# Which heads' row maxima are computed a stage ahead in a four-batch decoder layer

## The reference

```python
Q = (decoder_input @ W_q).reshape(B, Sd, HEADS, HEAD_DIM)      # 16 heads of 16
K = (encoder_output @ W_k).reshape(B, Se, HEADS, HEAD_DIM)
V = (encoder_output @ W_v).reshape(B, Se, HEADS, HEAD_DIM)
scores = jnp.einsum('bqhd,bkhd->bhqk', Q, K) / jnp.sqrt(jnp.float32(HEAD_DIM))
attn = jax.nn.softmax(scores, axis=-1)                         # maximum over 512 keys, per query
out = jnp.einsum('bhqk,bkhd->bqhd', attn, V).reshape(B, Sd, E)
return out @ W_o + b_o
```

## Time and profile before

| | |
|---|---|
| median of 3 runs | 544.41 us (543.29 to 546.53) |
| the profiled execution | 544.57 us |
| its span | 542.8 us |
| VectorE, ACT, POOL busy | 71%, 54%, 40% |
| stage 0 (first exponential to that of the next) | 98.5 to 209.0 us |
| stage 1 | 209.0 to 324.1 us |
| stage 2 | 324.1 to 424.3 us |
| stage 3 | 424.3 to the end of its slots near 512 us, then the tail |

### The profile page before, as it was taken

One profiled execution on the slowest core, in us unless ns is written; L12 is line 12 of the kernel. 1 busy time (PEld: TensorE's weight loads), 2 busy tenths in 40 slices (PEclk: granted clock), 3 DMA queues, 4 the chain that ended last, 5 costly groups with the idle time before them and its releaser, 6 DMA issues. The chain is left out here.

```text
span 542.8 us, 6272 instructions
## 1 busy us (share of the span) xinstructions
PE 458.3 (84%) x1931; PEld 188.2 (35%) x1931; DVE 384.6 (71%) x640; ACT 292.3 (54%) x516; POOL 215.4 (40%) x213
## 2 busy tenths in 40 slices
PE   8997889889795978899878889888988878787984
PEld 3432523324231213353332323443422332233453
DVE  4888878673777696577997896798557668732385
ACT  4145440552754563845757656546866434687434
POOL 5559793720358575321678772422000011000000
PEclk9999989988989889999999989998989978999998
DMA  7566460621758206034755032220501410000011
GB/s 219 212 178 168 141 174 4 154 56 33 189 135 209 62 17 150 19 79 120 174 139 123 0 95 73 80 58 3 147 19 37 90 50 2 2 0 2 1 39 40
DMA packets 26512, 47.33 MB, mean 87 GB/s; under 512 B 5456, under 2 KB 16368, under 8 KB 26480
## 3 DMA queue, kind: packets, MB, share of 16 engines
q1 hardware_dynamic: 23360, 39.86, 27.6%
q10 hardware_dynamic: 3120, 7.08, 5.3%
HBM read 35.19 MB, written 9.96 MB: 83 GB/s over the span
## 5 line engine op out<-in xcount | busy, mean ns | idle before, releaser
L1529 DVE TENSOR_REDUCE MX<-bank 128x1 f32<-128x512 f32 x256 | 166.5, 681 | 108.1 <-PE bank L637 103.3
L1138 ACT ACTIVATE PT<-bank 128x512 f32<-128x512 f32 x256 | 147.0, 597 | 121.7 <-PE bank L646 111.2
L637 PE MATMUL bank<-KS,QS 96*128 96x512 bf16 x240 | 93.6, 397 | 38.0 <-DVE MX L1529 28.3
L646 PE MATMUL bank<-QS,KS 99*128 99x512 bf16 x256 | 97.9, 393 | 19.6 <-ACT PT L1138 17.9
L1830 POOL TENSOR_TENSOR W<-qT,W 128x512 f32<-128x512 f32 x48 | 61.6, 1287 | 37.6 <-DVE W L1446 26.0
L660 PE MATMUL bank<-PT,Vs 128*32 128x512 f32 x512 | 73.5, 648 | 1.5 <-ACT PT L1138 0.8
L646 PEld LDWEIGHTS bank<-QS,KS 99*128 99x128 bf16 x256 | 24.2, 98 | 106.1 <-issue 53.3
L637 PEld LDWEIGHTS bank<-KS,QS 96*128 96x128 bf16 x240 | 23.6, 98 | 98.9 <-DVE MX L1529 62.0
L1861 POOL TENSOR_TENSOR MP<-MX,zero 128x16 bf16<-128x16 f32 x15 | 4.4, 292 | 115.7 <-DVE MX L1529 76.0
L1816 POOL TENSOR_TENSOR W<-kT,W 128x512 f32<-128x512 f32 x32 | 45.3, 1419 | 6.7 <-ACT kT L993 6.7
L1446 DVE TENSOR_TENSOR_SCAN W<-bank,W 128x512 f32<-128x512 f32 x32 | 38.7, 1210 | 0.0
(11 more groups left out here) (216 smaller groups left out, 707.2 us busy)
## 6 DMA issues: line engine op xcount, KB each, us to landing
W<-v_rows SPq DMA_DIRECT2D x12, 512.0 KB, 6.3
W<-v_rows ACTq DMA_DIRECT2D x12, 512.0 KB, 6.4
k_parts<-parts SPq DMA_DIRECT2D x24, 128.0 KB, 2.4
KS<-k_parts SPq DMA_DIRECT2D x16, 192.0 KB, 3.6
q_parts<-parts SPq DMA_DIRECT2D x24, 128.0 KB, 2.6
QS<-q_parts SPq DMA_DIRECT2D x16, 192.0 KB, 3.6
cT<-in_cT SPq DMA_DIRECT2D x4, 512.0 KB, 3.9
xtok<-in_x SPq DMA_DIRECT2D x4, 512.0 KB, 5.5
```

The source lines that it names most:

```text
L637: pe.matmul(bank(n)[:, :], QS[0:NS, h, i * P:(i + 1) * P], KS[0:NS, h, :], start=True, stop=True).then_inc(filled(n), 1)
L646: pe.matmul(bank(name)[:, :], KS[0:NR, h, kt * P:(kt + 1) * P], QS[0:NR, h, :], start=True, stop=True).then_inc(filled(name), 1)
L1138: act.activation(PT[:, n % 2, j, :], bank(name)[:, :], ACT.Exp).then_inc(emptied(name), 1)
L1529: dve.tensor_reduce(MX[:, NT * h + i:NT * h + i + 1], bank(n)[:, :], AX.X, ALU.max).then_inc(emptied(n), 1)
```

## The change

Before, LAG = 6 heads of the next batch had their maximum tiles in slots 10 to 15 of the stage ahead; the other ten had them in slots 0 to 9 of their own. In stage 0 the heads 4 to 15 had them there, since the prologue makes those of heads 0 to 3 only. After, LAG = 4: heads 0 to 3 in slots 10 to 14 of the stage ahead, and heads 4 to 15 in slots 0 to 9 of every stage, dealt as in stage 0 before.

```diff
-LAG = 6
+LAG = 4
...
-NEXT_MAXIMA = dealt("o", 10, (2, 4, 4, 4, 5, 5), range(LAG))
-MAXIMA = {s: {**dealt("b", 0, (4, 5, 6, 5, 6, 2, 5, 2, 3, 2), range(LAG, H)), **NEXT_MAXIMA} for s in STEPS}
-
-MAXIMA[0] = {**dealt("b", 0, (5, 7, 8, 7, 6, 3, 5, 2, 3, 2), range(4, H)), **NEXT_MAXIMA}
+MAXIMA = {**dealt("b", 0, (5, 7, 8, 7, 6, 3, 5, 2, 3, 2), range(LAG, H)), **dealt("o", 10, (2, 4, 4, 4, 2), range(LAG))}
+MAXIMA = {s: MAXIMA for s in STEPS}
```

## The result

The changed kernel takes 560.7 us (median of 4 runs, 559.69 to 561.05) against 545.5 for the kernel before in the same runs: ratio 1.0304, 95% interval 1.0259 to 1.0349. The forecast, 553.1 with a range of 547.2 to 556.8, had the direction and about half of the size. Medians are of all executions; ratios leave out the slow ones, more than 1.5% above the fastest of their kernel. The profiled span is 558.7 us against 542.8, 15.9 more where the sum had 8.7.

A forecast was written before the change was run, and what follows sets the result against it. Neither TensorE (84% busy) nor VectorE (71%) is full, so order and waits were taken to bound the kernel. The sum was 544.57 + 10.7 (starts) - 2.0 (ends) = 553.3, so 553.1 for the median; range 547.2 to 556.8.

The forecast's parts named there:

- the starts' term: Slots 0 to 5 of stages 1 to 3: 24 added tiles cost 2.9 + 3.8 + 4.0 = 10.7 us.
- Longer stalls at transposes may fall to the lower level (1.2 GHz) more often; I leave that in the range: TensorE's clock at the stage ends: might drop more often behind stalls; left in the range, no size in the sum.
- rival (b): Ends get worse: maxima's DMA takes 4.33 instead of 2.96 in stages 0 and 1, lower clock; 556.8 us, chance 0.09.
- Ends: Slots 14 and 15 of stages 0 to 2: gains 1.4 and 0.8, loss 0.2, together 2.0 us less.
- the chain: Slot 15: head 3's last maximum, POOL, transpose, copy, DMA, next stage's first score tile; needs 5.9 us whatever VectorE does.
- the 2.0 that the prediction set aside: Skill's fixed DMA cost, about 2.0 us; using it would make the sum 4.2 us less; stage 2's 4.33 spoke against.
- the two prices: Cost of a moved tile: 0.22 us if reductions find gaps, 0.68 if none; 5.3 to 16.3 us for 24.
- y0: Key point in slots 1 and 2, waiting for normalised OT by DMA; later by 0.7, 1.5 and 1.9 us in stages 1 to 3.
- Nothing after the starts is tied to a clock of its own: Slots after the starts: the starts' delay was expected to reach the end of the stage.
- (a): Starts: added maxima find gaps in VectorE, 5.3 - 2.0 = +3.3, 547.7 us; chance 0.12.
- (d): Exchange: what leaves the ends returns at the starts; within 2.7 us, 544.4 us; chance 0.10.
- (c): Ends shrink by VectorE's time, 13.3 us in all against 10.7 at the starts; 541.8 us, chance 0.05.

The follow-up runs named there:

- noend: Kernel before without the 24 maxima of heads 4 and 5 in batches 1 to 3, m3.3 where it was: 543.15 us against 543.93, ratio 0.9969.
- early: Changed kernel with m3.3 in slot 13, POOL's parts at (14, 0), the transpose at (14, 3): 560.6 us against 542.05 before, ratio 1.0345.
- nostart: Changed kernel without the 24 maxima of heads 4 and 5 in batches 1 to 3: 558.18 us against 543.93 before, ratio 1.0225.
- ends: `noend` with the change's deal of the heads ahead, so the last tiles of head 3 stand later: 548.46 us against 545.25 before, ratio 1.0053.
- only1: Kernel before with heads 4 and 5 moved for batch 1 only (end of stage 0, start of stage 1): 549.67 us against 542.05, ratio 1.0113.
- only2: Kernel before with heads 4 and 5 moved for batch 2 only (end of stage 1, start of stage 2): 550.05 us against 542.05, ratio 1.0135.
- only3: Kernel before with heads 4 and 5 moved for batch 3 only (end of stage 2, start of stage 3): 550.75 us against 542.05, ratio 1.0162.
- keep33: Changed kernel with m3.2 and m3.3 at (14, 0) and (14, 1), as in the kernel before: 559.69 us against 543.73 before, ratio 1.0296.
- warm: Changed kernel with unread matmuls, six before the transpose and five before the next stage's first score tile: 562.54 us against 543.93 before, ratio 1.0343.
- late33: Kernel before with m3.3 at (14, 3) and the first three tiles of head 4 one place up: 553.8 us against 543.73, ratio 1.0181.

## Why the prediction was wrong

The direction was right, and so were the place and the mechanism of the starts' term. The step that failed is the last of the sum: "Longer stalls at transposes may fall to the lower level (1.2 GHz) more often; I leave that in the range". It entered the sum at nothing, and it is 6.9 us of 16.4 (4.4 to 8.8 with slopes of 0.25 to 0.5), with the reservations on this split above. The mechanism was named rightly: 13.3 of the 17.4 us more at the lower level lie in slots 14 and 15, and the level fell at all three transposes. It had about 1 us in rival (b), where it was a term for every end. By place, the 7.2 us between 15.9 and the sum's 8.7 are 3.0 at the ends (+1.0 instead of -2.0), 1.4 at the starts (12.1 instead of 10.7) and 2.8 in the rest, which the sum had at nothing.

Ends, forecast -1.4, -0.8 and +0.2 up to the V matmuls. V0 comes 208.51 - 196.61 = 11.90 us after the start of slot 14 in stage 0, where it was 209.52 - 197.40 = 12.12, so -0.2. In stage 1 (324.63 before) it is -0.4, from these two rows of the changed kernel's timeline, and stage 2 is unchanged within 0.2:

```profile
325.99 0.29 PE L626 MATMUL bank<-identb,MP 128*128 128x128 bf16 x1 [1.39 <-POOL MP L1865]
...
330.11 1.89 PE L597 MATMUL bank<-xwv,cT 128*128 128x256 f32 x8
```

Together -0.6 instead of -2.0, and +1.0 over slots 14 and 15. Most of the miss is stage 0: m3.3 came at 202.41 instead of 201.9 and the transpose at 205.07 instead of 204.35, although slot 14 began 0.8 us earlier than before. That the chain and not VectorE sets the ends is supported by `noend` and `early`. (b)'s late DMA did not come: 2.5 us from issue to use in stage 0 and 3.2 in stage 1 (the sum had at most 2.96), below the 4 that it needed. In stage 2 it took 4.11; none of the three is near the 2.0 that the prediction set aside.

V0 of stage 1 took 1.6 us more at the lower level; that is in the start of stage 1.

Starts, forecast 10.7: measured 12.1 over slots 0 to 5 (4.28, 3.30, 4.50 against 2.9, 3.8, 4.0; the last takes slots 2 and 3 "as in stage 2" at 1.9, where stage 2 has 0.5 + 1.6 = 2.1, which changes nothing). Stage 1's granted clock is a little lower (0.96 against 1.00) and holds that 1.6; stage 3's is higher (0.94 against 0.87). On the whole the windows have no more of the lower level than before, so the sum is schedule. The price of a tile was bracketed rightly, and the choice between the two prices came out near the mark: 12.1 us for 24 tiles is 0.50 a tile. What I did not see is how unlike the places are: `nostart`, with the same 40 tiles a stage as `ends` but in the change's full slots 2, 3 and 5, costs more (5.9 us at equal clock, and 9.8 us of median span). y0 came 2.1 us later against its stage's start in stage 1 (forecast 0.7; 1.6 of it is V0 at the lower level), 1.5 in stage 2 (1.5) and 3.5 in stage 3 (1.9). Its rows in stages 1 and 2:

```profile
232.41 1.97 PE L597 MATMUL bank<-xwd,x1T 128*128 128x256 f32 x8 [0.56 <-DMA x1T<-OT]
...
353.36 1.96 PE L597 MATMUL bank<-xwd,x1T 128*128 128x256 f32 x8
```

In stage 3 the normalise is 3.2 us later against its start (forecast 1.8), with four maxima ahead of it in one run, where the kernel before has three:

```profile
446.18 2.48 DVE L1527 TENSOR_REDUCE MX<-bank 128x1 f32<-128x512 f32 x4 [0.18 <-PE bank L635]
448.58 0.68 DVE L1537 TENSOR_TENSOR OT<-OT,den 128x512 f32<-128x512 f32 x1
```

The kernel before:

```profile
434.90 1.92 DVE L1529 TENSOR_REDUCE MX<-bank 128x1 f32<-128x512 f32 x3
```

"Nothing after the starts is tied to a clock of its own" failed too: slots 6 to 15 without a moved tile gained and lost up to 1.7 us each, +3.7 in all with the tail. Slot 6 of stage 2 (-1.17) and slot 14 of stage 3 (+1.63) changed as stretches at the lower level fell elsewhere. Slot 6 of stage 1 (+1.69) did not: its granted clock is 1.00 in both kernels, and it is 1.7 longer in `only1` too and unchanged in `only2` and `only3`, so this is the start's own cost, carried one slot beyond where the sum ended.

Rivals: (a) and (d) are out by the starts, (c) by `noend`. What stays open is why the time at the lower level, as a median over executions, stays so high when the stalls at the transposes are gone (`early` 70.1, `keep33` 66.9, `warm` 70.1), though in their profiled executions slots 14 and 15 have 5.6, 4.1 and 6.8 us of it against the change's 20.1. The kernels at 65 us and more have either m3.3 late or the denser starts, but `late33` with 61.8 and the change with 62.0, which has both, show that the two do not add. Whether a placement exists that has the clock of the kernel before wasn't found.

## What to carry to other kernels

When a kernel's time is set by the order of work, put TensorE's clock into the sum as a term of its own: take the time at the lower level and its price from repeated executions, and do not read it from one profile alone, since executions of one kernel differ in it by more than most edits are worth. A moved tile cost 0.50 us at the starts here, more than twice TensorE's 0.22 and less than VectorE's 0.68, and not the same in every slot. Of a chain that crosses a stage's end, ask first where its last producer goes: moved back by two quarters of a slot it cost more here (5.1 us, `ends` against `noend`) than eight tiles fewer at each end gave (0.8, `noend` against the kernel before, not told from none).

## What the runs showed of the hardware

- Executions of one kernel differ by 15 us of 542, and the mean granted clock (0.938 to 0.971) orders them at 0.39 us of span for each us at 1.2 GHz.
- Kernels that do less work did not run at a higher clock: without 24 maxima 78.7 and 68.8 us at the lower level (`nostart`, `ends`) against 44.4, so the work left out did not shorten the time. `noend`, with the same work left out and m3.3 early, had 47.7.
- At the ends of stages 0 to 2 the lower level began beside the transpose of the maxima at 15 of the 18 places where TensorE had waited 1.38 to 2.25 us before it, and at 1 of the 33 with a wait of 0.86 us or less (all 17 profiled executions).
- Eleven matmuls that nobody reads at each such end took the time at the lower level in slots 14 and 15 from 20.1 to 6.8 us, but not that of the whole execution (`warm`, 72 us).
- The end of stage 2, at 1.00 in the earlier trace rows, ran at 0.60 after one maximum had moved by two quarters (`late33`), with 3.9 us more of TensorE's busy time for the same 35 matmuls.
